# Small factors and one wide intermediate of VectorE's wide operations move into PSUM banks of their own

## The reference

```
x = layernorm(x + L0(x, edges))     # hyperbolic attention, one weight per edge
x = layernorm(x + L1(x, src, dst))  # two convolutions
x = layernorm(x + L2(x, edges))     # attention with 4 heads
x = layernorm(x + L3(x, edges, edge_attr))  # attention with 1 head, edges in both directions
```

```
ex        = exp(e - segment_max(e, row)[row])
attention = ex / segment_sum(ex, row)[row]
weighted  = sqrt(c0) * attention[:, None] * log_h[col]
att_log_h = segment_sum(weighted, row)
h_prime   = tanh(..) * z / ..       # z = elu(att_log_h), scaled back onto the ball
```

```
logits = leaky_relu(s_node[src] + d_node[dst] + e_all)
z      = exp(logits - segment_max(logits, dst)[dst])
out    = segment_sum(z / denom[dst] * (x @ W)[src], dst)
```

## Time and profile before

| | us |
|---|---|
| median of 3 runs | 7980.62 |
| lowest, highest | 7980.48, 7987.24 |
| the profiled execution's own time | 7990.91 |
| its span | 7989.2 |

### The profile page before, as it was taken

One profiled execution on the slowest core, in us unless ns is written; L12 is line 12 of the kernel. 1 busy time (PEld: TensorE's weight loads), 2 busy tenths in 40 slices (PEclk: granted clock), 3 DMA queues, 4 the chain that ended last, 5 costly groups with the idle time before them and its releaser, 6 DMA issues. The chain is left out here.

```text
span 7989.2 us, 77514 instructions
## 1 busy us (share of the span) xinstructions
PE 2985.7 (37%) x14049; PEld 2378.1 (30%) x14049; DVE 5563.0 (70%) x16528; ACT 2917.5 (37%) x6586; POOL 5200.0 (65%) x5145
## 2 busy tenths in 40 slices
PE   4776700211111116777756634454400000362322
PEld 1222200211111116666646634444300000252221
DVE  6667687877767757777879969999634444463764
ACT  3555523433333334444434436666500000121211
POOL 0003774777777767777666547777567777777677
PEclk9888855555555557888856655555555555675555
DMA  8884217111111115555579944444321111663321
GB/s 103 112 115 98 69 18 64 27 26 25 25 25 25 25 35 154 169 176 178 167 254 308 311 139 146 147 154 147 125 56 45 45 45 44 141 225 108 97 92 61
DMA packets 786583, 864.06 MB, mean 108 GB/s; under 512 B 469875, under 2 KB 483427, under 8 KB 779804
## 3 DMA queue, kind: packets, MB, share of 16 engines
q1 hardware_dynamic: 572556, 684.47, 30.1%
q0 software_dynamic: 163408, 175.42, 10.5%
q10 hardware_dynamic: 50240, 0.60, 0.6%
HBM read 419.15 MB, written 480.23 MB: 113 GB/s over the span
## 5 line engine op out<-in xcount | busy, mean ns | idle before, releaser
L164 POOL DMA_INDIRECT T<-slot_at,home_row x393 | 433.5, 1103 | 814.9 <-DVE home_row L728 676.1
L1244 POOL DMA_INDIRECT e_other<-X,index x392 | 426.4, 1088 | 179.2 <-issue 117.8
L1232 POOL DMA_INDIRECT e_ahead<-XA,index x392 | 417.4, 1065 | 178.8 <-issue 118.9
L3032 POOL DMA_INDIRECT e_got<-G,index x392 | 370.2, 944 | 244.1 <-issue 112.3
L1892 POOL DMA_INDIRECT e_mine<-T,index x392 | 394.6, 1007 | 203.0 <-issue 114.3
L3661 POOL DMA_INDIRECT out_rows<-e4s_out,index x392 | 419.0, 1069 | 165.3 <-issue 118.8
L2383 PE MATMUL e_turned<-ident,e_own_x 128*128 128x128 f32 x196 | 54.6, 434 | 1233.9 <-DVE e_own_x L1971 1233.9
L1904 POOL DMA_INDIRECT X<-e_row,index x392 | 421.4, 1075 | 125.3 <-issue 118.8
L3470 POOL DMA_INDIRECT rows<-X,index x392 | 398.1, 1015 | 129.9 <-issue 129.9
L1255 POOL DMA_INDIRECT XA<-e4d_sent,index x392 | 393.2, 1003 | 119.4 <-issue 118.8
L1244 POOL DMA_INDIRECT e4d_other<-X,index x392 | 375.0, 957 | 136.1 <-issue 118.2
(11 more groups left out here) (695 smaller groups left out, 13110.3 us busy)
## 6 DMA issues: line engine op xcount, KB each, us to landing
XA<-e_n_xa SPq DMA_DIRECT2D x49, 1056.0 KB, 5.2
SUMS<-e_state SPq DMA_DIRECT2D x49, 1056.0 KB
e4n_n_xa<-XA SPq DMA_DIRECT2D x49, 1056.0 KB, 5.3
X<-e_n_row SPq DMA_DIRECT2D x49, 576.0 KB
X<-pl_x SPq DMA_DIRECT2D x98, 268.0 KB, 2.2
e_n_x<-X SPq DMA_DIRECT2D x49, 536.0 KB
B<-e_n_b SPq DMA_DIRECT2D x49, 528.0 KB
e_n_b<-B SPq DMA_DIRECT2D x49, 528.0 KB, 6.7
```

Of the source, the lines that this page charges most:

```text
L164: gp.indirect_dma_start(out=words, out_offset=bass.IndirectOffsetOnAxis(ap=home_row[:, t:t + 1], axis=0), in_=slot_at[:, t:t + 1], in_offs ...
L1232: gp.indirect_dma_start(out=ahead[:, b, j, :], out_offset=None, in_=g.XA[0:SLOTS, :], in_offset=bass.IndirectOffsetOnAxis(ap=index_of(g, 0 ...
L1244: gp.indirect_dma_start(out=other[:, h, j, :], out_offset=None, in_=others[:, :], in_offset=bass.IndirectOffsetOnAxis(ap=index_of(g, s, 1, ...
```

## The change

PSUM has 8 banks of 2 KB per partition, and each tile below has a bank to itself. TensorE writes none of the new ones, apart from `at_end`, which joins two small tiles of the end of the layer 0 stage in one bank to free another.

In layer 0 the two shifts, the factors of `products`, `shares` and `on_ball`, the row sum of `centred`, the inverse root and both weights of `pay_out` go to a PSUM tile `factors`. The second half of `big` and `hp` share a PSUM tile `second`. VectorE gets four small copies (two shifts, the first weight back into SBUF because `other_y` is in PSUM, the inverse root) and a wait behind each kind. In the one-head sum the pay factor and both rises are copied to PSUM, and `looped` lies there. In the node stage the share is written to PSUM, and the inverse root is copied there. In the last edge stage ScalarE's exponential is cut into three, of which two write to PSUM, `own_pay` and the shares lie in PSUM, and the inverse root is copied there.

```diff
 # attend_edges, kind "edge"
+        if kind == "edge":
+            factors, looped = ps("factors", [P, 3, J]), ps("looped", [P, J, D])
+            pay_factor, rises_of_ends = factors[:, 0, :], factors[:, 1:, :]
...
-                    rise = [logs[:, b, i, 0:count].unsqueeze(2) for i in range(2)]
+                    rise = [rises_of_ends[:, i, 0:count].unsqueeze(2) for i in range(2)]
...
+                    sums_dve.done(v.tensor_copy(rises_of_ends[:, :, 0:count], logs[:, b, :, 0:count]), "rises")
...
+                    need("rises")
...
-                        acc.done(v.tensor_tensor(pay[:, :, :], ot[:, :, 2:], ex[:, b, 1, :, :].to_broadcast([P, J, D]), ALU.mult), "pay")
+                        acc.done(v.tensor_copy(pay_factor, ex[:, b, 1, :, 0]), "factor")
+                        v.wait_ge(acc.sem, acc.after(n, "factor"))
+                        acc.done(v.tensor_tensor(pay[:, :, :], ot[:, :, 2:], pay_factor.unsqueeze(2).to_broadcast([P, J, D]), ALU.mult), "pay")
 # attend_edges0
-        spread, carried = ps("spread", [P, P]), ps("carried", [P, D + 2])
+        at_end, second = ps("at_end", [P, P + D + 2]), ps("second", [P, J, D])
+        spread, carried = at_end[:, 0:P], at_end[:, P:]
+        factors = ps("factors", [P, 10, J])
+        own_shift, other_shift, own_factor, other_factor, share_factor, ball_factor, total, inverse_root = (factors[:, i, :] for i in range(8))
+        weights = factors[:, 8:10, :].rearrange("p a j -> p j a")
...
-                    copied.done(v.tensor_tensor(own_x[:, h, :, :], mine[:, h, :, 0:D], mine[:, h, :, SHIFT:SHIFT + 1].to_broadcast([P, J, D]), ALU.add))
+                    v.tensor_copy(own_shift, mine[:, h, :, SHIFT])
+                    shifts.done(v.tensor_copy(other_shift, other[:, h, :, SHIFT]))
+                    v.wait_ge(shifts.sem, shifts.after(n))
+                    copied.done(v.tensor_tensor(own_x[:, h, :, :], mine[:, h, :, 0:D], per(own_shift), ALU.add))
...
-                    dve.done(v.tensor_tensor(big[:, 1, :, :], other_y[b][:, :, :], per(tmp[:, 10, :]), ALU.mult), "t2")
+                    dve.done(v.tensor_tensor(second[:, :, :], other_y[b][:, :, :], per(tmp[:, 10, :]), ALU.mult), "t2")
...
-                    dve.done(v.tensor_tensor(big[:, 0, :, :], big[:, 0, :, :], big[:, 1, :, :], ALU.add), "ma")
+                    dve.done(v.tensor_tensor(big[:, :, :], big[:, :, :], second[:, :, :], ALU.add), "ma")
...
-                    acc.done(v.tensor_tensor(pay[:, :, :], other_y[b][:, :, :], per(weights[:, :, 0]), ALU.mult), "pay")
+                    acc.done(v.tensor_copy(pay_factor[:, :], weights[:, :, 0]), "factor")
+                    need("factor")
+                    acc.done(v.tensor_tensor(pay[:, :, :], other_y[b][:, :, :], per(pay_factor[:, :]), ALU.mult), "pay")
...
-                    ball.done(v.tensor_tensor(hp[:, 0:count, :], z[:, 0:count, :], per(q[:, 10, :], count), ALU.mult), "hp")
+                    ball.done(v.tensor_tensor(second[:, 0:count, :], z[:, 0:count, :], per(ball_factor[:, 0:count], count), ALU.mult), "hp")
...
-                    centre.done(v.tensor_reduce(q[:, 0, :], rows, AX.X, ALU.add), "total")
+                    centre.done(v.tensor_reduce(total[:, 0:count], rows, AX.X, ALU.add), "total")
...
+                    inverse_roots.done(v.tensor_copy(inverse_root[:, 0:count], norm_t[:, b, 4, 0:count]))
+                    v.wait_ge(inverse_roots.sem, inverse_roots.after(n))
...
-                    x1_made.done(v.tensor_tensor(row[:, h, 0:count, 0:D], y[:, b, 0:count, :], per(norm_t[:, b, 4, 0:count], count), ALU.mult))
+                    x1_made.done(v.tensor_tensor(row[:, h, 0:count, 0:D], y[:, b, 0:count, :], per(inverse_root[:, 0:count], count), ALU.mult))
 # finish_nodes
+        n_p, factors = sb("n_p", [P, 2, 2, GROUP, D]), ps("factors", [P, 2, G2])
+        n_share, n_inverse_root = factors[:, 0, :], factors[:, 1, :]
...
+                    n_inverse_roots.done(v.tensor_copy(n_inverse_root, n_small[:, 3, :]))
+                    v.wait_ge(n_inverse_roots.sem, n_inverse_roots.after(n))
 # finish_edges
+        turned, own_pay = ps("turned", [P, 4, P]), ps("own_pay", [P, J, D])
+        factor, own_factor, shares = ps("factor", [P, T]), ps("own_factor", [P, T]), ps("shares", [P, T + J])
+        share, inverse_root = shares[:, 0:T], shares[:, T:]
...
+                    inverse_roots.done(v.tensor_copy(inverse_root, small[:, 3, :]))
+                    v.wait_ge(inverse_roots.sem, inverse_roots.after(n))
...
-                prep_act.done(a.activation(ex[:, :, :], ex[:, :, :], ACT.Exp), "ex")
+                prep_act.done(a.activation(ex[:, 0, :], ex[:, 0, :], ACT.Exp), "ex")
+                prep_act.done(a.activation(factor[:, :], ex[:, 1, :], ACT.Exp), "factor")
+                prep_act.done(a.activation(own_factor[:, :], ex[:, 2, :], ACT.Exp), "own_factor")
```

82 lines of the change are left out of this document (40 added, 42 removed).

## The result

The changed kernel takes 7846.32 us, the median of four runs (7843.39 to 7849.19); the kernel before took 7983.35 us on the same chip (four runs, 7980.48 to 7987.24). The ratio is 0.9828, with a 95% interval from 0.9811 to 0.9845: 137 us less, where 145 were forecast, and a time 10 us above the 7836 that was predicted. Of the profiled executions, which the sum was made for, it is 7990.9 to 7849.0 us, or 142 us less.

What follows compares the result with a forecast made beforehand. POOL's pace of indirect DMA issues was taken to bound four stages. Delays of 148.2 us removed, less 2 for lead-ins and 1.2 for remaining operations, gave 145 us: 7836 us after a 10.3 us offset, range 7822 to 7852.

Steps and rivals of the forecast that it cites:

- The bound: Layer 0, one-head sum, node and last edge stages: time is the number of indirect DMAs times POOL's pace.
- What goes: Issue delays beside wide VectorE operations with two SBUF inputs, in four stages: 148.2 us removed, bounds 131 to 162.
- The weighing of an operation by the square of its length: Layer 0's remaining short sums: eight of 64 elements count an eighth of one of 512; 71.7 of 79.6 us goes.
- Why layer 0 goes: Layer 0: ten of eleven wide operations get one PSUM input and so stop delaying POOL, 71.7 us.
- Rival A: Layer 0: meeting times lock, so `elu` could meet an issue in all 49 chunks, 25 us; about 7858 us; chance 0.10.
- What is added: VectorE's added copies, 0.20 us each with wait, 0.8 us per layer 0 chunk, hidden under its waits in the steady part.
- Lead-ins: Stage starts, where POOL waits for VectorE's first results: about 1 us in the last edge stage, 1 us in the others together.
- The move to PSUM: Wide VectorE operations reading or writing PSUM instead of SBUF take the same time (692 ns); priced at nothing.
- rival B: Wide operations: a PSUM operand makes them slower, 152 us more in layer 0 alone; about 8098 us; chance 0.02.
- From the sum to the time: Whole kernel: 145 us off the profiled 7990.9 gives 7845.9; less 10.3 for its offset above the median, 7836 us.
- D: Layer 0: a chain through PE and ScalarE becomes the limit, half of 71.7 us is lost; 7872 us; chance 0.04.
- C: Long issues have another cause, such as the wide operations' writes; nothing goes, lead-ins stay; 7983 us; chance 0.02.

Runs made afterwards that it cites:

- The twin: The changed kernel with all its new PSUM operand tiles put back in SBUF, same copies, waits and order: 7959.77 us, ratio 0.9962 to the kernel before.
- either placement: The changed kernel as it is (7846.32 us), and with four dependent idle copies ahead of layer 0's first wide addition (7846.48 us, ratio 0.9822).
- the probe without waits: The changed kernel plus a second pass of 392 node-stage gathers beside blocks of 96 back-to-back VectorE operations; some 500 us longer, not compared.
- the last two probes: The changed kernel plus 392 more node-stage gathers beside VectorE groups of four, multiplied or added, behind spacers of changing length; no total given, issues at most 1.45 us.

## Why the prediction was right, and where it wasn't

**The bound.** Right: in all four stages the time followed POOL's issues, and POOL's idle time stayed at its own 0.30 us.

**What goes.** By stage: layer 0 71.7 us forecast and 66.1 measured (68.2 by the means: 203 less 29 ns, times 392), one-head sum 12 and 11.5, node stage 27.8 and 28.0, last edge stage 36.7 and 37.7. The weighing of an operation by the square of its length came out near: the 29 ns left in layer 0 are 11.4 us, against the 7.9 that it leaves. That is 3.5 of the 5.6 us that layer 0 fell short. Counted over the trace, `elu` has 5.8 of the 11.4 us, where 7.2 were given to it, and the running sums 0.8; the rest is spread over many issues that last a few ns longer than the median, which the sum took to go with the wide operations.

**Why layer 0 goes.** This step was incomplete, though its number stood. The prediction took the excess before for a standing price of ten operations, and its loss for the work of the PSUM operands alone. The twin shows that 47.6 of the 66.1 us go with the shifted meetings alone; before, an issue began under `own_x` nearly once in every chunk. That the number stood is no luck: with PSUM operands 28 or 29 ns are left in either placement, so the stage falls by about the excess before, whichever of the two causes would have taken it first. Rival A had the mechanism, meeting times that lock, but the prediction looked for it only in the kernel after, for `elu`. It was in the kernel before. A sign of it was to be had in the trace of before: in 49 chunks 45 issues begin under the same operation, of 0.70 us, where by chance, with an issue every 1.3 us, some 26 would. For the other three stages the step was right: with the operands in SBUF and the same instructions, nothing of the gain is left.

**What is added.** Right: the copies cost nothing that the end sees. VectorE's wait for landings in layer 0 fell by 107.5 us (72 + 39 = 111 forecast), in the last edge stage by 50.5 (47). In the node stage it fell by 28.1 us, where 37.6 were counted: POOL came forward by 28.0, and the 49 copies didn't put VectorE's end back at all: it stands 426 us behind POOL's first gather of the stage in both traces. Lead-ins: the gap ahead of the last edge stage grew from 46.1 to 46.6 us, not by 1.

**The move to PSUM.** Right, against rival B: L2084 and L2086, the counterparts of the earlier trace rows, have 691 and 686 ns, and the 1024 elements of L3518 1.22 us, for 1.23 in the earlier trace rows. The extra 65 ns that the Trainium skill gives in "VectorE: DVE Perf Modes", section "The TRN2 errata", showed nowhere; in the probe without waits the operation with a PSUM input took less, 673 for 699 ns.

**From the sum to the time.** By spans 142.0 us went, of 145. The rest of the 10 us between 7836 and 7846 is the step from one execution to the median. The prediction took off the 10.3 us by which the profiled execution of before stood above the median as if the kernel after had the same offset; the one after stood 2.6 us above its own. That offset was scatter of runs, and no more than a middle value should have been taken from it.

**The rivals.** A gave no `elu` in every chunk (21 long issues in the whole stage, not 49). B and D fell by the durations and by VectorE's waits. C fell by the node and last stages of the twin. The sentence of the Trainium skill that would have made C true ("SBUF — State Buffer", section "Who interferes with whom": that an operation on two tensors takes only the read side, which descriptor generation is inferred not to need) disagrees with 1150 against 947 ns. Three other rules that the Trainium skill has there agree: that an operation with at most one SBUF input doesn't contend, outside the modes in which VectorE takes both ports (943 and 947 ns), that a reduction doesn't (947), and that a copy can (1083).

## What to carry to other kernels

Where GpSimd's issues of indirect DMAs set the pace, look at their mean against their median, and at what VectorE runs when a long one begins; an operation of 512 elements on two SBUF tensors can cost an issue half a microsecond here, and one small factor, copied once into a PSUM bank of its own, ended that. Before you credit the cure, run the twin with the same instructions and the operands left in SBUF: two engines with regular rhythms meet at fixed places, and any edit that shifts one of them can gain or lose tens of microseconds that have nothing to do with its purpose. And the cure ends where the next bound begins: in the heads 72 us of relief for GpSimd were worth about 10.

## What the runs showed of the hardware

- Two engines fall into step. Back to back, 96 operations on two SBUF tensors ran at 0.624 us each, half of POOL's 1.249, with almost no delay of the issues; with a PSUM input they ran at 0.598. With a wait behind each the step is 0.727 us and the issues come every 1.45, each 0.2 us longer. What an operation costs a neighbour can't be read from one rhythm alone.
- For copies the place of the result counts, other than for operations on two tensors: inside SBUF 426 to 432 ns, with issues of 1083 ns back to back and 975 with gaps, into PSUM 694 ns and issues of 944.
- An issue that one wide operation on two SBUF tensors holds up ends 0.82 us in the median after that operation has ended (a scatter 0.85), wherever in it the issue began. Four adds in a row in the heads hold an issue until the last has ended (2.23 to 3.22 us in all), where ten kinds of four in the last two probes never did (1.45 us at most). It wasn't settled why.
